# Local attention: Newton step and clip of the inverse norms of queries and keys on GpSimd

## The reference, cut to what matters

```python
x = x + 0.5 * ffn(layernorm(x))      # two layers of local attention and gated MLP
x = x + attn(layernorm(x))           # global attention with a memory
x = x + 0.5 * ffn(layernorm(x))

# in each layer of ffn, per token and head (8 heads of 64):
l2norm(t) = t / clip(norm(t), 1e-12)
q = l2norm(q) * q_scale; k = l2norm(k) * k_scale
q, k = rotary_xpos(q, k)
o = softmax(8 * q @ k.T within windows of 64 and the window before) @ v
x = x + o @ wo; x = x + mlp(layernorm(shift(x)))
```

## Time and profile before

| what | us |
|---|---|
| median of 3 runs | 1976.98 (1975.87 to 1977.96) |
| span of the profiled execution | 1971.5 |
| PE, DVE, ACT, POOL busy in it | 1906.8, 1623.9, 1483.3, 916.0 |

### The profile page before, as it was taken

One profiled execution on the slowest core, in us unless ns is written; L12 is line 12 of the kernel. 1 busy time (PEld: TensorE's weight loads), 2 busy tenths in 40 slices (PEclk: granted clock), 3 DMA queues, 4 the chain that ended last, 5 costly groups with the idle time before them and its releaser, 6 DMA issues. The chain is left out here.

```text
span 1971.5 us, 52907 instructions
## 1 busy us (share of the span) xinstructions
PE 1906.8 (97%) x18490; PEld 1129.9 (57%) x18490; DVE 1623.9 (82%) x5453; ACT 1483.3 (75%) x4089; POOL 916.0 (46%) x549
## 2 busy tenths in 40 slices
PE   7999999999999989999999999899999999999998
PEld 4777763577775343434434367437777646777743
DVE  6999964899994579999999769779999548999844
ACT  5999993799997253777777754469999837999962
POOL 2787860578781040000000046337878406787700
PEclk9999999999999997999999999999999999999999
DMA  6121220112120040111111000002212201121301
GB/s 188 43 48 43 48 60 6 35 43 49 42 66 23 6 152 28 41 42 42 42 42 43 19 5 2 2 21 47 49 43 47 55 6 42 42 49 42 70 12 43
DMA packets 76106, 85.08 MB, mean 43 GB/s; under 512 B 17139, under 2 KB 50499, under 8 KB 75715
## 3 DMA queue, kind: packets, MB, share of 16 engines
q1 hardware_dynamic: 75647, 81.68, 16.3%
q10 hardware_dynamic: 196, 0.02, 0.0%
HBM read 21.14 MB, written 8.39 MB: 15 GB/s over the span
## 5 line engine op out<-in xcount | busy, mean ns | idle before, releaser
L304 ACT ACTIVATE probs<-probs,negmax 128x128 f32<-128x128 f32 x1024 | 399.8, 396 | 23.2 <-DVE negmax L377 22.1
L2083 ACT ACTIVATE gprobs<-ps_global 128x1024 f32<-128x1024 f32 (+3 forms) x384 | 291.4, 810 | 124.3 <-PE ps_global L1548 101.2
L259 POOL TENSOR_TENSOR rot<-rot 128x1024 f32<-128x1024 f32 x128 | 302.5, 2363 | 145.6 <-DVE rot L347 145.6
L265 POOL TENSOR_TENSOR qk<-rot,cnorm 128x1024 f32<-128x1024 f32 x128 | 243.8, 1905 | 120.1 <-POOL rot L259 89.5
L272 POOL TENSOR_TENSOR probs<-probs,iden 128x1024 f32<-128x1024 f32 x128 | 242.9, 1898 | 120.0 <-DVE iden L385 120.0
L1778 DVE TENSOR_REDUCE maxes<-ps_global 128x1 f32<-128x512 f32 (+2 forms) x384 | 222.0, 637 | 10.2 <-PE ps_global L1511 6.5
L377 DVE CUSTOM_DVE_ANT_0 probs<-ps_attn,masks 128x128 f32<-128x128 f32 x1024 | 226.2, 285 | 0.0
L1506 PE MATMUL ps_global<-kq 48*128 48x512 bf16 (+3 forms) x768 | 196.7, 345 | 7.2 <-DVE maxes L1778 1.8
L304 ACT ACTIVATION_READ_ACCUMULATOR probs<-probs,negmax 128x1 f32 x1024 | 197.0, 192 | 0.0
L345 DVE TENSOR_TENSOR rot<-ps_attn,rotary 128x512 f32<-128x512 f32 x256 | 174.8, 683 | 1.8 <-PE ps_attn L171 1.6
L239 PEld LDWEIGHTS ps_attn<-probsT,v_first 128*64 128x64 f32 x2048 | 118.1, 136 | 98.1 <-ACT probsT L325 94.3
(11 more groups left out here) (212 smaller groups left out, 4585.0 us busy)
## 6 DMA issues: line engine op xcount, KB each, us to landing
v_first<-v_second SPq DMA_DIRECT2D x256, 128.0 KB, 2.3
hs<-z_a SPq DMA_DIRECT2D x256, 32.0 KB, 1.9
ln<-z_b SPq DMA_DIRECT2D x56, 128.0 KB, 2.4
kq<-split_scratch SPq DMA_DIRECT2D x64, 96.0 KB
kq<-split_scratch SPq DMA_DIRECT2D x64, 64.0 KB
split_scratch<-parts SPq DMA_DIRECT2D x8, 384.0 KB, 4.1
split_scratch<-gprobs SPq DMA_DIRECT2D x6, 384.0 KB, 3.9
x_tok<-in_x_dram SPq DMA_DIRECT2D x4, 512.0 KB, 6.4
```

Source lines behind the costliest of these rows:

```text
L259: nc.gpsimd.tensor_tensor(a, a, b, ALU.add).then_inc(C["rot_sum"], 1)
L265: nc.gpsimd.tensor_tensor(qk[:, k % 2, :].rearrange("p (h d) -> p h d", d=DH), rot_a[:, k % 2, :, :], cnorm[:, k % 2, :].unsqueeze(2).to_b ...
L304: last = nc.scalar.activation(probs[:, k % 2, slot, :], probs[:, k % 2, slot, :], ACT.Exp, scale=-1.0, bias=negmax[:, k % 2, slot:slot + 1 ...
L2083: nc.scalar.activation(probs[:, step % RING, 2 * p:2 * p + 2, 0:w], ps[:, S0 + 2 * p:S0 + 2 * p + 2, 0:w], ACT.Exp).then_inc(C["p2_exp"], 1)
```

## The change

The Newton step and the clip go from DVE to GpSimd, where they stand at the head of `gp_rotary_scale`, behind the rotary sum of the same tile. GpSimd gets five instructions, since the form with two operations on two tensors that DVE used becomes separate products and one multiply-and-add: n = r*r; n = n*ssq; n = -0.5*n + 1.5; c = n*r; c = min(c, 1e12). All calls of `dve_clip_norm` go, in the bodies, at the end of a layer, in the opening and between the layers. The wait for the ssq buffer asks for `newton_done` of two tiles back in place of `norm_log`, since GpSimd reads ssq later than ACT. The semaphore `newton` counts 3 per tile and not 2.

```diff
+        def gp_clip_norm(gp, wait, i, k):
+            r, n, c = inorm[:, k % 2, :], newton[:, k % 2, :], cnorm[:, k % 2, :]
+            wait("norm_inv", i, k)
+            nc.gpsimd.tensor_tensor(n, r, r, ALU.mult).then_inc(C["newton"], 1)
+            wait("newton", i, k, 0, 3, 2)
+            nc.gpsimd.tensor_tensor(n, n, ssq[:, k % 2, :], ALU.mult).then_inc(C["newton"], 1)
+            wait("newton", i, k, 0, 3, 1)
+            nc.gpsimd.tensor_scalar(n, n, -0.5, 1.5, ALU.mult, ALU.add).then_inc(C["newton"], 1)
+            wait("newton", i, k, 0, 3)
+            nc.gpsimd.tensor_tensor(c, n, r, ALU.mult).then_inc(C["newton_done"], 1)
+            wait("newton_done", i, k)
+            nc.gpsimd.tensor_scalar(c, c, NORM_MOST, None, ALU.min).then_inc(C["norm_ready"], 1)
+
         def gp_rotary_scale(gp, wait, i, k):
+            gp_clip_norm(gp, wait, i, k)
             wait("rot_sum", i, k)
             wait("norm_ready", i, k)
             wait("k_turned", i, k, 2)
...
         def dve_ssq(dve, wait, i, k):
             wait("k_squared", i, k)
-            wait("norm_log", i, k, 2)
+            wait("newton_done", i, k, 2)
...
-        def dve_clip_norm(dve, wait, i, k):
-            r, n = inorm[:, k % 2, :], newton[:, k % 2, :]
-            wait("norm_inv", i, k)
-            nc.vector.tensor_tensor(n, r, r, ALU.mult).then_inc(C["newton"], 1)
-            wait("newton", i, k, 0, 2, 1)
-            nc.vector.scalar_tensor_tensor(out=n, in0=n, scalar=-0.5, in1=ssq[:, k % 2, :], op0=ALU.mult, op1=ALU.mult
-                                           ).then_inc(C["newton"], 1)
-            wait("newton", i, k, 0, 2)
-            nc.vector.scalar_tensor_tensor(out=n, in0=n, scalar=1.5, in1=r, op0=ALU.add, op1=ALU.mult
-                                           ).then_inc(C["newton_done"], 1)
-            wait("newton_done", i, k)
-            wait("qk_ready", i, k, 2)
-            nc.vector.tensor_scalar(cnorm[:, k % 2, :], n, NORM_MOST, None, ALU.min).then_inc(C["norm_ready"], 1)
...
                 if ahead(i, k, 0):
                     dve_probsT(dve, wait, i, k)
-                if ahead(i, k, 3):
-                    dve_clip_norm(dve, wait, *tile_of(i, k + 3))
...
             hides(0, 22, 23)
-            dve_clip_norm(dve, wait, *t(1, 0))
-            dve_clip_norm(dve, wait, *t(1, 1))
             hides(0, 23, 24)
```

More of the change, by code:

```diff
@@ L1016, in attention_end @@
                 dve_probsT(dve, wait, *t(layer, 28))
-                dve_clip_norm(dve, wait, *t(layer, 31))
                 dve_inv(dve, wait, *t(layer, 29))
@@ L1060, in _ @@
             dve_rotate(dve, wait, 1, *t(0, 1))
-            dve_clip_norm(dve, wait, *t(0, 0))
             dve_ln_scale(dve, -1, 5)
@@ L1066, in _ @@
             dve_ln_scale(dve, -1, 7)
-            dve_clip_norm(dve, wait, *t(0, 1))
             dve_rotate(dve, wait, 1, *t(0, 2))
@@ L1071, in _ @@
             dve_max(dve, wait, *t(0, 0))
-            dve_clip_norm(dve, wait, *t(0, 2))
             dve_rotate(dve, wait, 1, *t(0, 3))
@@ L1114, in _ @@
             dve_max(dve, wait, *t(1, 0))
-            dve_clip_norm(dve, wait, *t(1, 2))
             dve_rotate(dve, wait, 1, *t(1, 3))
@@ L1158, in local_attention_pass @@
     once = {name: DEPTH * TILES for name in ATTENTION_SEMS if name not in ("newton", "max_done")}
-    C.close(newton=2 * DEPTH * TILES, max_done=HEADS * DEPTH * TILES, pass_set=2, ln_low=DEPTH, ln_high=DEPTH,
+    C.close(newton=3 * DEPTH * TILES, max_done=HEADS * DEPTH * TILES, pass_set=2, ln_low=DEPTH, ln_high=DEPTH,
             **{f"ln_in{m}": DEPTH * (32 if m == 3 else 64) for m in range(4)},
```

## The result

| kernel | median us | ratio to before (95% interval) |
|---|---|---|
| before | 1976.65 | |
| changed | 1997.24 (1996.06 to 1999.11) | 1.0106 (1.0092 to 1.012) |

The change costs 20.6 us, about 1%.

The account below looks back on a forecast made before the run. The prediction took a loop through GpSimd and a held DVE Newton instruction, 7.59 us a tile, as the bound. Span 1971.5 + 1.1 (pace 7.60) + 2.6 (edges) = 1975.2, plus 5.5 to the median: 1981.0 us given, range 1962 to 2011.

Parts of the forecast that it names:

- four-engine loop: Per tile: output projection, residual, sum of squares, Ln, Exp, GpSimd's Newton chain, scaling, transposes; forecast as the pace, 7.60 us.
- C: Time on GpSimd from the first new instruction's start to the scaling's start, forecast at 1.44 us per tile.
- decisive 1.43: Length in us of GpSimd's added chain below which the change gains and above which it loses: 7.59 - 6.16.
- PE's floor: Shortest pace that TensorE's own row of work allows per tile, forecast at 7.43 to 7.50 us.
- The loop of the kernel before: Reciprocal, softmax scaling, rotary sum, held Newton instruction on DVE, rotations, reciprocal: claimed to set the pace of 7.59 us.
- 6.16 us outside the chain: Sum per tile of the steps through PE, DVE, ACT and GpSimd other than the added Newton chain.
- GpSimd's 6.04: GpSimd's own work per tile without the added chain: scaling 1.86, softmax scaling 1.86, sum 2.36, less 0.04 overlap.
- Doubling DVE's steps: Pricing GpSimd's five instructions at twice DVE's 0.21 us spacing: 2.1 us, loop 8.26, time 2055 us; chance 0.05.
- dear chain: Rival: GpSimd's added chain takes 1.52 to 1.9 us, slower, 2011 us at 1.7; chance 0.24.
- the tie: Main case: added chain of 1.33 to 1.52 us, period 7.49 to 7.68, time 1969 to 1990 us; chance 0.40.
- cheap chain: Rival: added chain of 1.33 us or less, TensorE's own row sets the pace, 1962 to 1970 us; chance 0.22.
- The edges: Extra time at two layer changes (1.0 us each) and two openings (0.3 us each), together 2.6 us.

Follow-up runs that it names:

- e8_one_port: The kernel before with its three Newton instructions and the clip on VectorE replaced by one-column reductions (Newton step and clip not computed): 1968.77 us.
- e10_max_dve: The kernel before, Newton step on VectorE, clip replaced by a second reduction that clamps the sum of squares: 1969.01 us, ratio 0.9965.
- e11_before_ssq_first: The kernel before with the sum of squares put ahead of the residual in VectorE's order: 1975.74 us, ratio 0.9999.
- e4_one_input: The kernel before with its three Newton instructions on VectorE replaced by one-input products with 1.0 (Newton step not computed): 1975.23 us, ratio 0.9999.
- e1_ssq_first: The changed kernel with the next tile's sum of squares put ahead of the residual in VectorE's order: 1986.13 us, ratio 1.0054 to the kernel before.
- e2_no_clip: The changed kernel without the clip, the last of the five small GpSimd instructions: 1968.97 us, ratio 0.9969 to the kernel before.
- e9_max_gp: The changed kernel with four small GpSimd instructions, sum of squares ahead of the residual, clip replaced by a clamping reduction on VectorE: 1968.96 us.
- e7_dve_clamp: The kernel before, Newton step on VectorE, clip replaced by a tensor-scalar clamp of the sum of squares on VectorE: 2062.24 us, ratio 1.0435.
- e3_one_more: The changed kernel with the clip done twice on GpSimd, six small instructions: 2040.95 us, ratio 1.0332 to the kernel before.
- e5_bare: The changed kernel with the clip alone left on GpSimd and the Newton step not computed: 1967.24 us, ratio 0.9953 to the kernel before.

## Why the prediction was right in its direction, and where it was off

The change was forecast slower and within the range, and it is. The four-engine loop that was named as the pace is the pace. But the direction rested on the 0.01 us between C at 1.44 and the decisive 1.43: with an error of the same 0.14 us to the other side the kernel would have fallen to PE's floor and been faster. The direction was luck; the chances, 0.49 for slower, said as much.

- *The loop of the kernel before* (7.59 through the held Newton instruction): right, shown by e8_one_port and e10_max_dve, which shorten or open it, and by e11_before_ssq_first, which leaves it. The condition that I gave for the hold, two SBUF inputs, was too narrow: e4_one_input.
- *6.16 us outside the chain in the four-engine loop*: right to 0.01 us in two kernels (7.74 - 1.58, 8.07 - 1.92), and e1_ssq_first shows that the loop is the one named. GpSimd's 6.04 was right too (7.62 - 1.58).
- *C*: the term that was mis-sized. 1.44 was forecast, 1.58 measured. The tensor-tensor instructions take 0.215 to 0.222 us, not the 0.175 of the straight line through 128 and 1024 columns: 3 x 0.045 = 0.13 of the 0.14. The dependent gaps are 0.08 to 0.09, not 0.075 (0.05 more), and the tensor-scalars together 0.03 less. The estimate by spacing, 1.39, was farther off: the starts are 0.28 to 0.31 us apart, against 0.24 worked out from the 0.48 of the earlier trace rows. Doubling DVE's steps gave 2.1, far too much; the small GpSimd instructions start 0.30 us apart against DVE's 0.21, not quite half as much again. 0.14 x 112 is 16 us, the whole distance between 1981.0 and 1997.24.
- *The case*: what came is the low end of the dear chain (C from 1.52), which had 0.24, not the tie that I put first with 0.40. The decisive value, 1.43, was right within 0.01, and C lies above it.
- *PE's floor*: 7.53, where I had 7.43 to 7.50. The time of a cheap chain would have been 1969 (e2_no_clip, e9_max_gp), the upper end of the 1962 to 1970 that I gave.
- *The edges*: forecast 1.0 us late at the change of layer. Measured, PE waits 1.14 us there for the second tile's scaling (below, against the earlier trace rows). The bodies give (7.74 - 7.59) x 112 = 17 us, with the 2.6 of the edges 19.4, against 20.6 measured. In the traces the two changes of layer cost 1.3 us each and the two openings -0.25 and 0.13, 2.5 in all: the 2.6 is right in sum, though I gave 1.0 and 0.3. One term I had left out: the last interval of each layer's bodies was 6.87 us in the kernel before and is 7.74 now, so those four tiles lose 0.87 and not 0.15 us, 2.9 us more in all. With it the sum is 22.3; the medians lie 20.6 apart and the spans 24.7.

```profile
374.72 1.09 PE L193 MATMUL ps_attn<-ident,qk 128*128 128x128 f32 x8 [1.14 <-POOL qk L280]
```

## What to carry to other kernels

An engine whose busy share is 46% of the whole span can be busy 82% of the stage that counts, and its idle time there, 0.79 + 0.67 us a tile, was less than the chain it was given: list, for each engine, what it does per tile and what the last input of each step is, and put the sum of every loop beside the pace, before and after the move. Price a chain of small dependent instructions from start to start and with a margin, because on the new engine it is the fixed part that counts, and a line through large shapes doesn't show it. Where one engine is held by another, look at the form of the instruction first: here a reduction in place of a tensor-scalar in the same place took 0.19 us for 1.27 and brought the pace from 8.27 to 7.53, and with this clamp as a reduction it made no difference on which of the two engines the Newton step stood.

## What the runs showed of the hardware

- DVE's tensor-tensor, two-tensor and float32 tensor-scalar instructions on SBUF stand still until GpSimd's running instruction ends (0.49 to 0.50 us in L360 of before and of e4_one_input, where the same instruction without a hold takes 0.17 in e7_dve_clamp; 1.75 to 1.76 us in L365 at the change of layer, where a reduction takes 0.17; 1.27 and 1.32 us for the clamp). The rows show this where DVE starts second. Reductions from SBUF, of 1024, 32 and 16 columns, run beside it (1.21, 0.19 and 0.16 us; e7_dve_clamp, e10_max_dve, e8_one_port). That one-input tensor-scalars belong to the first group I had not expected.
- GpSimd takes 0.20 to 0.25 us for an instruction of 128x16, and the next small one that depends on it starts 0.28 to 0.33 us after its start (changed kernel, e3_one_more).
- TensorE starts the loads of 128x128 weights 0.18 us behind the last 64x64 ones where no other engine is late (e5_bare, e8_one_port).
